# Four products that nothing reads, added on PE to each step of dense pairs of a graph network kernel

## The reference

```python
# layer 0: three hops
for _ in range(3):
    msg = (x * norm_out[:, None])[src]
    agg = segment_sum(msg, dst, N)
    x = 0.5 * (agg * norm_in[:, None]) + 0.5 * h0
y = layernorm(h0 + x @ W.T)
# layer 1: attention over the edges
edge_feat = concatenate([y[src], y[dst]], axis=1)
h = relu(edge_feat @ W1 + b1)
w = sigmoid(h @ W2 + b2)[:, 0]
agg = segment_sum(w[:, None] * y[src], dst, N)
out = layernorm(y + layernorm(y + agg) * gamma + beta)
```

## Time and profile before

| | |
|---|---|
| median of 3 runs | 1668.03 us (1667.2 to 1671.71) |
| the profiled execution | 1669.32 us, of which its span is 1667.6 us |
| busy share of the span | PE 67%, PEld 51%, DVE 63%, ACT 32%, POOL 42% |
| granted TensorE clock, mean | 0.675 of full speed |
| indirect DMAs of POOL | 576, 75.53 MB in all |

### The profile page before, as it was taken

One profiled execution on the slowest core, in us unless ns is written; L12 is line 12 of the kernel. 1 busy time (PEld: TensorE's weight loads), 2 busy tenths in 40 slices (PEclk: granted clock), 3 DMA queues, 4 the chain that ended last, 5 costly groups with the idle time before them and its releaser, 6 DMA issues.

```text
span 1667.6 us, 37005 instructions
## 1 busy us (share of the span) xinstructions
PE 1117.0 (67%) x11236; PEld 857.4 (51%) x11237; DVE 1044.1 (63%) x4680; ACT 528.7 (32%) x1635; POOL 693.1 (42%) x744
## 2 busy tenths in 40 slices
PE   2666668999991325666666766776766776666771
PEld 2666656888870213544544544554544554544551
DVE  7988877645561364664675675675675664674667
ACT  1555551100320001332332332332332332332346
POOL 4000009200447646455555455445445445445511
PEclk9999998999995555565655555555555555555565
DMA  2000000000126323223223223223223223223311
GB/s 69 1 0 0 0 1 1 1 1 3 49 54 189 93 62 95 70 77 92 74 75 92 76 72 93 75 72 94 74 71 96 74 68 94 73 72 94 88 32 41
DMA packets 74421, 102.49 MB, mean 61 GB/s; under 512 B 30568, under 2 KB 50460, under 8 KB 74268
## 3 DMA queue, kind: packets, MB, share of 16 engines
q0 software_dynamic: 27648, 75.53, 15.7%
q1 hardware_dynamic: 46620, 25.02, 5.5%
HBM read 93.98 MB, written 6.52 MB: 60 GB/s over the span
## 4 chain that ended last, share of the span: by engine, by line
PE 39%; DVE 32%; issue 15%; another core or an unknown queue 8%; ACT 3%; DVEq 1%; POOL 1%; DMA 1%; ACTq 0%; SPq 0%; POOLq 0%
PE bank L1574 10%; PE bank L1616 7%; DVE region L1148 6%; PE bank L1612 5%; DVE stage L875 4%; PE bank L1512 3%; DVE region L1206 3%; DVE region L1218 2%; PE bank L1677 2%; PE bank L1631 2%; DVE region L1216 2%; PE bank L1514 2%; DVE region L1197 2%; DVE region L1226 1%
## 5 line engine op out<-in xcount | busy, mean ns | idle before, releaser
L779 POOL DMA_INDIRECT region<-src_split,region x576 | 572.8, 994 | 519.2 <-PE bank L1631 323.9
L1148 DVE SCALAR_TENSOR_TENSOR region<-bank,vec 128x128 f32<-128x128 f32 x576 | 133.0, 287 | 324.1 <-PE bank L1616 160.2
L1612 PE MATMUL bank<-region,ident 128*128 128x512 f16 x288 | 144.4, 603 | 173.1 <-issue 100.0
L1900 ACT ACTIVATE ws<-zs,b2s 128x4 f32<-128x4 f32 x144 | 42.8, 297 | 616.4 <-DVE region L1148 436.8
L1574 PE MATMUL bank<-U,region 128*128 128x256 f16 (+1 forms) x1875 | 226.2, 276 | 12.4 <-DVE U L1009 6.9
L1574 PEld LDWEIGHTS bank<-U,region 128*128 128x128 fp8e4 x1875 | 183.0, 98 | 44.4 <-DVE t L1044 6.1
L1677 PE MATMUL bank<-region 128*128 128x64 f16 x832 | 80.5, 236 | 143.7 <-DVE region L1218 141.3
L1616 PEld LDWEIGHTS bank<-region 32*128 32x128 f16 x1152 | 104.2, 130 | 115.4 <-issue 115.4
L1835 ACT CAST region<-bank 128x500 f32 x202 | 119.7, 593 | 96.1 <-PE bank L1514 73.3
L1677 PEld LDWEIGHTS bank<-region 128*128 128x128 f16 x832 | 48.7, 119 | 187.0 <-DVE region L1218 178.1
L1644 PE MATMUL bank<-ident,region 128*128 128x128 f16 x832 | 118.4, 293 | 32.7 <-issue 13.7
(11 more groups left out here) (270 smaller groups left out, 2529.1 us busy)
## 6 DMA issues: line engine op xcount, KB each, us to landing
region<-src_split,region POOLq DMA_INDIRECT x576
region<-in_dst_dram SPq DMA_DIRECT2D x144, 64.0 KB
U<-src_split SPq DMA_DIRECT2D x2, 1600.0 KB
region<-tgt_split SPq DMA_DIRECT2D x144, 16.0 KB
src_split<-y SPq DMA_DIRECT2D x25, 64.0 KB, 1.5
src_split<-pq SPq DMA_DIRECT2D x25, 64.0 KB, 1.7
tgt_split<-pq SPq DMA_DIRECT2D x25, 64.0 KB, 2.0
out_dram<-region SPq DMA_DIRECT2D x5, 256.0 KB, 2.3
```

Of the source, the lines that this page charges most:

```text
L779: nc.gpsimd.indirect_dma_start(out=G[:, p * TPS + i, :], out_offset=None, in_=src_split, in_offset=bass.IndirectOffsetOnAxis(ap=listed[n % ...
L1148: z = nc.vector.scalar_tensor_tensor(out=spare[i][:, :], in0=bank[q % 2][:, i * P:(i + 1) * P], scalar=0.0, in1=vec[:, W2, :], op0=ALU.max ...
L1612: nc.tensor.matmul(bank[q % 2][:, 0:m * P].rearrange("p (t k) -> p t k", k=P), ident16[:, :], G[:, first:first + m, half * D:(half + 1) * ...
```

## The change

After each step with 4 <= j < 26, PE issues four more products of 384 columns: `ident16` against columns 128 to 511 of `iota`, written to columns 128 to 511 of bank 7. Nothing reads them. They wait for nothing and signal nothing. There are 22 such steps in a turn (both steps of slots 2 to 12) and 8 turns, so 176 places and 704 products (and as many weight loads). In an even step they stand ahead of `sums`, in an odd step ahead of the sort's piece if there is one and of the next batch's `scored`.

```diff
+            def keep_busy(times):
+                for _ in range(times):
+                    nc.tensor.matmul(bank[7][:, D:4 * D], ident16[:, :], iota[:, D:4 * D], start=False, stop=True,
+                                     skip_group_check=True)
+
             def turn_pair(it, k):
...
                     spread_pair(it, j - 2)
                 if 0 <= j - 4 < BUCKETS:
                     sum_pair(it, j - 4)
+                if 4 <= j < BUCKETS:
+                    keep_busy(4)
```

## The result

The changed kernel takes 1744.98 us (median of four runs, 1741.64 to 1745.55) against 1668.04 for the kernel before beside it: a ratio of 1.045, with a 95% interval of 1.043 to 1.047, so 77 us slower. The forecast was 1718, in a range of 1675 to 1770, and slower; the measured time stands at the upper edge of the forecast's own band (1698 to 1745). In after, the lines behind `keep_busy` are shifted by five: its product is L1639, `turn_pair` L1649, `fetch_pair` L1667 to L1669, `spread_pair` L1682, `sum_pair` L1693 to L1695.

The account below looks back on a forecast made before the run. Neither PE nor DVE was full: a loop of waits, each handing over to the other. Half the low-clock cost less a third of the high-clock gain, 59 − 8 = 51 us, rounded to +50 on 1668.0, gave 1718; range 1675 to 1770.

Parts of the forecast that it names:

- A: Rival for the attention's turns: the clock stays low because pauses break PE's busy stretches; +118 us, 1786; chance 0.10.
- B: Rival for the attention's turns: the clock stays high and the products pay for themselves; -24 us, 1644; chance 0.10.
- DVE's chain at 1.05 us: Inside a slot: at the low clock the even step's group makes DVE's second score 1.0 to 1.05 us late.
- F1: First group of a slot, four products in the even step ahead of `sums`; 1.28 us of PE at the low clock.
- all-low terms: Cost of each hand-over into slots 3 to 13 with the clock always low: 0.4 to 2.3 us, 15.2 a turn.
- Half of the low-clock cost: Share taken over turns 1 to 8, as the clock rises often but doesn't hold: 59 of 118 us.
- F2: Second group of a slot, four products in the odd step ahead of the next `scored`; 1.28 us at the low clock.
- Room: Ahead of DVE's first score: its start less the end of `scored`, taken as absorbing PE delay; 1.05 us into slot 5.
- the unnamed waits keep their 4.3 us: DVE's waits for something the profile doesn't name, after `scored` had ended, were to stay at 4.3 us.
- all-low sum: Cost over all 8 turns if every group runs at the low clock: 118 us.
- The gain of 8 us: `scored` 0.8 us shorter at the high clock, mainly into slots 4, 8, 12; a third of 24 us was taken.
- C: Rival: groups fall mostly into cover, the first running at the high clock more often; +16 us, 1684; chance 0.16.

Follow-up runs that it names:

- e8: Against the kernel before: four products of 16 columns only after the odd step of slot 4, 32 in all; 1681.29 us, ratio 1.008.
- e3: The full change with all 704 products kept, but 16 columns each in place of 384; 1696.05 us, ratio 1.017 against the kernel before.
- e9: The kernel of e3 once more, all gathers kept, on a chip where the kernel before takes 1499.98 us; 1504.54 us, ratio 1.003.

## Why the prediction was right, and where it was off

**Sign, and the mechanism inside the slots: right.** The products cost PE's time where DVE waits for PE, and the clock rises without staying up. The mean clock of turn 4 is 0.72 (0.7 to 0.8 was forecast), PE is 5.9 us busier (at most 10), DVE as busy as before. A (+118) and B (-24) are both out: the clock of a turn is neither 0.55 nor 0.9.

**DVE's chain at 1.05 us: right.** L1206 is later by 1.04 us in the median where F1 and what follows ran at the low clock. By hand-over, the means over turns 1 to 7 against the all-low terms: into slot 8 1.1 (1.05), 9 1.31 (1.05), 13 1.28 (1.4), 5 1.76 (1.4), but 10 0.70 (1.5), 11 1.02 (2.3), 7 0.29 (1.35) and 12 -0.53 (0.4).

**The share at the low clock: too small for F1.** "Half of the low-clock cost" would be 46 us for F1 (11 × 8 × 1.05 / 2); it was 52 inside the slots, as 56 of its 88 groups ran low and only 29 high. The clock had been high where `scored` started and was low again at F1 in 37 of the 56, and in 25 of the 56 it fell in the very pause ahead of the first `spread_pair`; in 16 it was low throughout (worked out from the records of the clock). The Trainium skill ("TensorE: Matmul & The Clock Gate", section "HAM oscillation — how this bites in real kernels") describes the like for a loop that waits for a DMA: each piece of work behind the wait starts at the low clock. Here the wait is for DVE, and the trace agrees in those 25 slots, not in each. The forecast said that F1 and F2 stand just behind such pauses, and then used one half for both groups; of F2, 42 groups ran high and 31 low.

**"Room" that was none: the step that failed.** The forecast took DVE's start less the end of L1616 as room that a later `scored` could use up: 1.05 into slot 5. The row itself said that DVE sat idle for 2.62 us ahead of that start, so nothing else held it. It was late news: the signal of that `scored` is recorded at 1065.91, 1.06 us after the product's end. A little more on PE doesn't eat into it but can push `scored` past the moment, and then costs 1.44 us (e8). The same failing lies in "the unnamed waits keep their 4.3 us": each did (131.0 / 32 = 4.1), but there are 32 of them in place of 20. The all-low sum has 118 − 92 = 26 us for what lies beyond DVE's chain; that the 25.5 us between the slots come near it is chance, since nearly empty products (e3) make 31.1.

**The gain of 8 us: half of it.** Into slots 12 and 4, where `scored` starts on DVE's word, after is 2.8 and 1.5 us shorter between the slots (sums over the 8 turns), but into slot 8 it is 2.0 us longer. In after most `scored` of slots 3 to 13 start at the high clock, and between all slots the time still grew by 25.5 us, hardly less than with narrow products at the low clock (31.1). In slot 4 of turn 4 the faster `scored` had the 0.14 us next to the old distance, and the news came 1.18 us later. F1 has a hand in it: POOL's burst waits for L1631, and starts 5.97 us after the slot's start on PE (1094.28) where it started at 4.82 before (1061.64); the news came 4.33 and 4.30 us behind it. If the burst sets the moment, a faster `scored` behind a late burst gains nothing. That the distance is the same in both is measured; that the burst is its cause is argued.

**The sum.** 52.1 inside and 25.5 between make 77.6, against 46 + 13 - 8 = 51 forecast: 6 us from the clock's share, some 20 from what lies between. C (+16) falls with the first: F1 was not run at the high clock more often than the mean says, but less.

**Smaller misses.** PE's waits for L1218 and L1182 were to shrink. They grew from 126.6 to 169.8 us (148.7 from 700 to 1600 us) and stayed at 24 to 26. A likely reading, not tested, is that PE at the high clock is done sooner and waits the longer for the same DVE. DVE's named wait for L1616 was to grow and fell from 139.8 to 132.6; the unnamed one grew in its place. A turn is 10 us longer, not 6.

## What to carry to other kernels

Filler that is to keep TensorE's clock up belongs into a wait that ends on someone else's word, with an end before it: seven products a place there gave 9 us, while filler behind such a wait ran at the low clock in two of three cases and then made DVE's chain 1.04 us longer, for the 1.28 us that it takes. And the gain comes only where the reader hears of the faster product at once. Before taking the distance between a product's end and its reader's start as room, look at whether the reader was idle: if it was, the distance is a delay and may grow in a jump. And a wait that the profile can't name is worth comparing with the record of the product it should be for, and with the moment at which its semaphore was raised.

## What the runs showed of the hardware that was not expected

- DVE learned of a finished product late, mostly by 0.4 to 2.8 us after its recorded end, in 52 of 126 slots of before, most of them (43) 4.2 to 4.5 or 5.6 to 6.0 us after POOL began a burst of four indirect DMAs. On another chip none of 121 slots shows it.
- It is PE's signals that are late: 333 of 991 by over 0.3 us in before, 250 of the 284 whose product ended 2.0 to 5.5 us after such a burst began; no signal of DVE or ACT that can be paired with its end, and none on the other chip. That the bursts cause it isn't shown.
- The same kernel takes 1668 us on some chips and 1501 us on another (e3 and e9, one kernel on both: turn 0 takes 132.7 and 93.4 us, a later turn 127.7 and 108.8).
- 32 products of 16 columns, 0.15 us a group, cost 14 us; 704 of them, 88 a turn in one idle place, cost 11.5 us.
- 88 nearly empty products in a row took 5.6 us, with five pauses of 0.44 to 0.53 us that no other engine's work explains.
